# Attention over sorted edges: the first term of a quad's sum goes to PSUM by ScalarE, and VectorE's steps are joined over quads

## What is computed

```python
w_m = (efeat @ W_msg + b_msg).reshape(E, in_f, -1)
w_a = (efeat @ W_attn + b_attn).reshape(E, in_f, -1)
h_src = feat[src][:, :, None]
e1 = w_m * h_src
e2 = w_a * h_src
seg_max = jax.ops.segment_max(e2, dst, num_segments=N)
ex = jnp.exp(e2 - seg_max[dst])
denom = jax.ops.segment_sum(ex, dst, num_segments=N)
attn = ex / denom[dst]
ft = jax.ops.segment_sum(e1 * attn, dst, num_segments=N)
```

## Time and profile before

| | us |
|---|---|
| median of 3 runs (lowest to highest) | 8912.76 (8904.54 to 8920.91) |
| the profiled execution, its own time | 8910.58 |
| its span in the profile | 8908.9 |
| attention blocks (tops copied, first to last start) | 5804.2 to 8779.9 |

### The profile page before, as it was taken

The page is one execution under the profiler, slowest core; times in us unless marked ns, Lnnn a source line. Parts: engine busy times, 40 slices in busy tenths (PEclk is TensorE's granted clock), DMA queues, the critical chain, the costliest instruction groups (busy, mean ns, idle before and its releaser), DMA issues. The chain is left out here.

```text
span 8908.9 us, 135582 instructions
## 1 busy us (share of the span) xinstructions
PE 7159.9 (80%) x35152; PEld 4074.4 (46%) x35152; DVE 7506.5 (84%) x11807; ACT 4804.9 (54%) x7730; POOL 6381.3 (72%) x6335
## 2 busy tenths in 40 slices
PE   3888857888887088888888889488888888888884
PEld 3776744565565055555555555233333333333331
DVE  7999956788888388888888888499999999999997
ACT  5999956666775065665666556233333333333333
POOL 6777767777776677777777777377777777777774
PEclk9989967888888589999999999699999999999997
DMA  4222211111111111111111111122222222222223
GB/s 155 64 62 63 62 42 45 45 46 46 48 46 43 15 29 31 28 33 28 33 28 28 33 28 18 20 72 76 76 76 80 78 76 76 76 76 78 81 76 100
DMA packets 499695, 493.19 MB, mean 55 GB/s; under 512 B 181075, under 2 KB 396906, under 8 KB 498731
## 3 DMA queue, kind: packets, MB, share of 16 engines
q1 hardware_dynamic: 299595, 371.60, 12.4%
q0 software_dynamic: 199904, 119.78, 8.1%
HBM read 240.96 MB, written 249.95 MB: 55 GB/s over the span
## 5 line engine op out<-in xcount | busy, mean ns | idle before, releaser
L2524 POOL DMA_INDIRECT attn_got<-tab,attn_line x1760 | 1912.2, 1086 | 791.6 <-issue 503.5
L1982 POOL DMA_INDIRECT sheaf_got<-tab,sheaf_idx x1612 | 1702.7, 1056 | 488.5 <-issue 470.2
L2577 PE MATMUL attn_q<-attn_X,ident 128*128 128x512 f32 x3520 | 1718.0, 627 | 101.5 <-ACT attn_S L2657 92.5
L2071 PE MATMUL sheaf_acc<-sheaf_hot_hi,sheaf_wide 128*128 128x392 bf16 x6696 | 1355.1, 345 | 283.3 <-DVE sheaf_hot_hi L2274 281.5
L1508 POOL DMA_INDIRECT nnconv_got<-tab,nnconv_idx x1116 | 1081.4, 969 | 381.9 <-issue 321.6
L2577 PEld LDWEIGHTS attn_q<-attn_X,ident 128*128 128x128 f32 x3520 | 652.1, 198 | 1193.5 <-issue 1193.5
L2714 DVE TENSOR_TENSOR attn_T<-attn_w,attn_got 128x1024 f32<-128x1024 f32 x880 | 1052.8, 1217 | 152.0 <-PE attn_w L2568 116.7
L2657 ACT COPY attn_S<-attn_q 128x512 f32<-128x512 f32 x440 | 255.9, 582 | 1531.2 <-PE attn_q L2584 1531.2
L1173 POOL DMA_INDIRECT gcn_got<-tab,gcn_idx x868 | 827.6, 953 | 304.0 <-issue 277.1
L2071 PEld LDWEIGHTS sheaf_acc<-sheaf_hot_hi,sheaf_wide 128*128 128x128 bf16 x6696 | 655.8, 106 | 819.7 <-issue 491.1
L1267 PE MATMUL gcn_acc<-gcn_hot,pieces 128*128 128x512 f32 x2604 | 740.6, 442 | 196.7 <-ACT gcn_hot L1321 134.1
(11 more groups left out here) (508 smaller groups left out, 13676.9 us busy)
## 6 DMA issues: line engine op xcount, KB each, us to landing
sums<-attn_S SPq DMA_DIRECT2D x110, 1024.0 KB, 5.1
tops<-attn_S SPq DMA_DIRECT2D x110, 512.0 KB, 2.9
attn_got<-tab,attn_line POOLq DMA_INDIRECT x1760
sheaf_got<-tab,sheaf_idx POOLq DMA_INDIRECT x1612
gcn_key<-src_key SPq DMA_DIRECT2D x62, 384.0 KB
gcn_blk<-src_blk SPq DMA_DIRECT2D x62, 384.0 KB
nnconv_got<-tab,nnconv_idx POOLq DMA_INDIRECT x1116
nnconv_key<-src_key SPq DMA_DIRECT2D x62, 256.0 KB
```

The lines of the kernel that those rows point to most:

```text
L1982: e.indirect_dma_start(out=got[at.b][:, j, D:D + T2], out_offset=None, in_=tab[2], in_offset=indices(idx[at.b], j)).then_inc(s_got[half][a ...
L2071: mm = e.matmul(pacc[k][:, 0:HH], wide[at.b][half][:, part, col, :], hot[:, k * HH:(k + 1) * HH], start=False, stop=False, skip_group_chec ...
L2524: e.indirect_dma_start(out=got[at.b][:, 4 * q + n, :], out_offset=None, in_=tab[3], in_offset=indices(ids[:, q, n, :], D + 2)).then_inc(s_ ...
L2577: e.matmul(to, ident[:, :], X[:, q, :, n, :], start=n == 0, stop=False)
```

## The change

ScalarE gets a new step, `begin_sum(at, q)`: it copies slot 0 of a quad's weights and weighted products from `X` straight into the bank `pq`. PE then adds only the slots 1 to 3 and the pass on top, with products that never begin a group (start=False); one opening product ahead of the stage starts the bank once. `s_open` and `s_begun` are the semaphores for it. DVE's `larger` over slots is one instruction for four quads where it was two; `below` and `product` are two instructions of two quads each where they were four of one, `below` as a TENSOR_TENSOR subtraction in place of a SCALAR_TENSOR_TENSOR; and their order around `back` changes.

```diff
             def quad_sum(at, q, between=None):
                 to = pq.rearrange("p (t c) -> p t c", t=2)
-                turn_wait(e, s_prod, at.of(QB, q + 1))
-                turn_wait(e, s_state, at.of(QB, q + 2))
-                for n in range(4):
-                    e.matmul(to, ident[:, :], X[:, q, :, n, :], start=n == 0, stop=False)
+                turn_wait(e, s_begun, at.of(QB, q + 1))
+                for n in range(1, 4):
+                    e.matmul(to, ident[:, :], X[:, q, :, n, :], start=False, stop=False, skip_group_check=True)
                     if between and n == 2:
                         between()
...
+            def begin_sum(at, q):
+                e.wait_ge(s_prod, at.of(2, q // 2 + 1))
+                if q > 0 or at.k > 0:
+                    e.wait_ge(s_state, at.of(QB, q + 2))
+                e.copy(pq.rearrange("p (t c) -> p t c", t=2), X[:, q, :, 0, :]).then_inc(s_begun, 1)
...
                 if at.k > 0:
                     put_state(prev, 1)
+                    begin_sum(prev, 2)
                     put_state(prev, 2)
+                    begin_sum(prev, 3)
...
                 tops_out(at)
                 if at.k < NBQ - 1:
                     passing(at.plus(1))
+                begin_sum(at, 0)
                 put_state(at, 0)
+                begin_sum(at, 1)
...
-            def below(q):
-                e.scalar_tensor_tensor(
-                    out=Tb[:, q, 0, :, :], in0=Tb[:, q, 0, :, :], scalar=1.0,
-                    in1=ptop[:, q, None, :].to_broadcast([P, 4, CH]), op0=ALU.mult, op1=ALU.subtract).then_inc(s_sub, 1)
+            def below(half):
+                q = slice(half * QB // 2, (half + 1) * QB // 2)
+                e.tensor_tensor(Tb[:, q, 0, :, :], Tb[:, q, 0, :, :],
+                                ptop[:, q, None, :].to_broadcast([P, QB // 2, 4, CH]),
+                                ALU.subtract).then_inc(s_sub, 1)
...
-                for q in range(QB - 2, -1, -1):
-                    n = back(q)
-                    below(q + 1)
-                    ch.wait(n)
+                n = back(2)
+                ch.wait(n)
+                n = back(1)
+                below(1)
+                ch.wait(n)
+                ch.wait(back(0))
...
                 below(0)
                 if more:
                     times(nxt, 2)
-                product(0)
                 e.wait_ge(s_scale, at.of(1, 1))
...
-                product(1)
+                product(0)
                 if more:
                     times(nxt, 3)
-                product(2)
-                product(3)
+                product(1)
```

More of the change, by code:

```diff
@@ L2457, in gnn_kernel @@
             s_carried, s_pass, s_at, s_mk, s_ids = seml("carried", "pass", "line_at", "mk", "ids")
+            s_begun, s_open = seml("begun", "open")
             s_copied, = seml("copied")
@@ L2549, in _ @@
                     e.wait_ge(s_w, 16 * 5 * (P // RW))
+                    e.matmul(pq[:, :], ident[:, :], Wc[:, :], start=True, stop=True).then_inc(s_open, 1)
                     def turned(at):
@@ L2583, in quad_sum @@
                         before = carried[:, :] if q == 0 else S[at.b][:, q - 1, CH:]
-                        e.matmul(pq[:, :], passes[at.b][:, q, :], before, start=False, stop=True).then_inc(s_quad, 1)
+                        e.matmul(pq[:, :], passes[at.b][:, q, :], before, start=False, stop=False,
+                                 skip_group_check=True).then_inc(s_quad, 1)
                     def step(at):
@@ L2609, in _ @@
                     e.sem_inc(s_state, 2)
+                    e.wait_ge(s_open, 1)
                     def line_index(at):
@@ L2633, in weights @@
                     def weights(at, q):
-                        e.wait_ge(s_sub, at.of(QB, QB))
+                        e.wait_ge(s_sub, at.of(2, 2))
                         if at.k > 0:
@@ L2692, in _ @@
                         put_state(At(NBQ - 1), q)
+                        if q < QB - 1:
+                            begin_sum(At(NBQ - 1), q + 1)
                 @block.vector
@@ L2707, in times @@
                         if q == 0 and at.k >= 2 and 0 in halves:
-                            e.wait_ge(s_prod, at.of(QB, -QB))
+                            e.wait_ge(s_prod, at.of(2, -2))
                         if q % 2 == 0 and 0 in halves:
@@ L2744, in back, with product @@
                                 in1=Sb[:, q, 0:CH], op0=ALU.add, op1=ALU.max))
-                        def below(q):
-                            e.scalar_tensor_tensor(
-                                out=Tb[:, q, 0, :, :], in0=Tb[:, q, 0, :, :], scalar=1.0,
-                                in1=ptop[:, q, None, :].to_broadcast([P, 4, CH]), op0=ALU.mult, op1=ALU.subtract).then_inc(s_sub, 1)
-                        def product(q):
-                            e.wait_ge(s_x, at.of(QB, q + 1))
+                        def below(half):
[3 more added lines that the diff above has]
+                                            ALU.subtract).then_inc(s_sub, 1)
+                        def product(half):
+                            q = slice(half * QB // 2, (half + 1) * QB // 2)
+                            e.wait_ge(s_x, at.of(QB, (half + 1) * QB // 2))
                             e.scalar_tensor_tensor(out=X[:, q, 1, :, :], in0=Tb[:, q, 1, :, :], scalar=1.0,
@@ L2759, in a_block @@
                         e.wait_ge(s_t, at.of(2 * QB, 2 * QB + 2))
-                        for q in range(0, QB, 2):
-                            n = ch.do(larger(two[:, q:q + 2, :, :].rearrange("p q n c -> p q (n c)"),
-                                             Tb[:, q:q + 2, 0, 0:2, :].rearrange("p q n c -> p q (n c)"),
-                                             Tb[:, q:q + 2, 0, 2:4, :].rearrange("p q n c -> p q (n c)")))
+                        n = ch.do(larger(two[:, :, :, :].rearrange("p q n c -> p q (n c)"),
+                                         Tb[:, :, 0, 0:2, :].rearrange("p q n c -> p q (n c)"),
+                                         Tb[:, :, 0, 2:4, :].rearrange("p q n c -> p q (n c)")))
                         if more:
@@ L2811, in _ @@
                         times(At(0), q)
-                    walk(e, NBQ, a_block, ch, 3 + QB + QB - 1, head=4)
+                    walk(e, NBQ, a_block, ch, 2 + QB + QB - 1, head=4)
                     e.wait_ge(s_state, NBQ * QB + 2)
```

## The result

| | median us | runs | profiled span us | mean granted clock | us per attention block |
|---|---|---|---|---|---|
| before | 8916.42 | 8904.54 to 8920.91 | 8908.9 | 0.897 | 27.30 |
| after | 9303.58 | 9298.46 to 9309.89 | 9296.7 | 0.854 | 30.69 |

The change makes the kernel slower, by a ratio of 1.0438 (95% interval 1.0425 to 1.045). The median of before is now over four runs. 9304 lies in the range of 9010 to 9320, 84 us above the 9220 that was forecast.

A forecast was written before the change was run, and what follows sets the result against it. The prediction took a loop of PE's stretch A and VectorE's stretch B as the bound. A 16.01, clock 1.75 and B 12.34 made 30.10 us a block against 27.30, +308 us: 9220, range 9010 to 9320 (0.80).

The forecast's parts named there:

- What bounds the kernel: Attention loop: A from t0 (end of `times(nxt, 2)`) to `times(.., 1)`, 14.84 us; B from there to next t0, 12.20.
- The first copy stands late: ScalarE's quad 0 copy (0.59 us) queues behind the pass matrices; PE starts at t0 + 4.94 instead of t0 + 1.56.
- The second copy: ScalarE's quad 1 copy, 0.59 us behind `put_state`; PE's shortened sum starts at t0 + 11.16, making A 16.01 us.
- The clock: PE's longer pauses leave its clock low in every block for 3.5 us of work, adding 1.75 us to A.
- VectorE in B: The new order of `back` and joined `below` lengthens VectorE's stretch B by 0.14 us, to 12.34.
- The sum: Attention block: 16.01 + 1.75 + 12.34 = 30.10 us against 27.30, +308 us over 110 blocks, 9220 in all.
- The three joins in A save 0.18 us of VectorE's readiness and no time: Joined `larger` and two joined `product` steps in A: VectorE ready 0.18 us earlier, no gain as PE is late.
- the third rival: ScalarE's first copy starts as its data come, at t0 + 2.85; block 27.24 us, 8904 in all; chance 0.05.
- That the clock stays high: PE's clock in attention stays high or as often high as before; block 28.35 us, 9026 in all; chance 0.18.
- That it stays low 5 us or more beyond PE's return, through quad 1's sum: PE's clock costs another 1.75 us a block; 9412 in all, 9316 if one block in two; chance 0.06.
- VectorE as the bound: VectorE bounds attention and PE follows, so joins and removed products gain 1.43 us a block; 8753 in all; chance 0.09.
- GpSimd was written off: GpSimd's gathers in the attention stage were taken as idle in part of each block, with no cost added.

The follow-up runs named there:

- the kernel without joined products: VectorE's joined maxima and `below` on the kernel before, with its four single-quad products kept and no ScalarE copies into the bank: 8910 us.
- joins only: VectorE's joined maxima, `below` and products and their new order on the kernel before, without ScalarE's copies; PE adds all four slots: 9279 us.
- The early copy: The changed kernel with `begin_sum(at, 0)` moved ahead of `tops_out` and `passing`: 9173 us.
- the two fastest kernels: Kernel before with `matrices(at.plus(2), 0)` behind the fourth product and two spare products in PE's pause, without and with ScalarE's copy for quad 1: 8806 and 8795 us.
- joins only with spare products: VectorE's joins without ScalarE's copies, on the kernel before, plus two spare identity products in each of PE's two pauses: 9095 us.
- the last kernel: The changed kernel with its first copy ahead of `tops_out` and `passing`, plus three and two spare products in PE's pauses: 9067 us.
- the moved matrices: Kernel before with `matrices(at.plus(2), 0)` behind the fourth identity product of quad 0 instead of the third: 8913 us; with two spare products, 8806 us.

## Why the prediction came out as it did

- *What bounds the kernel.* Right: a loop of PE's stretch A and VectorE's stretch B. Spare products on the kernel before gave 27.05, its block at full clock. That a shorter A gains down to VectorE's own time was confirmed only once the clock was held (26.26); without it the clock takes such gains back.
- *The first copy stands late.* Right in place and size: t0 + 4.85 for t0 + 4.94, 0.587 us for 0.59. Moving it gave 131 us.
- *The second copy.* Right: from the pass's end (7025.84) to `matrices` (7030.89) 5.05 us, forecast 4.95.
- *The clock.* Right in kind, too small in size: the term was 1.75 us a block and measured 2.29 in A (7.13 less 4.84). It was taken as "as long as it stayed low after it came back", 3.5 us. PE came back at 7014.01 and the clock rose at 7023.25, 9.2 us later: the products of `matrices(nxt, 3)` between two pauses did not raise it. Counted from that return, 3.5 us would have been over before quad 0's start at t0 + 4.94, and A would have lost nothing; the term fits only if the 3.5 us begin with quad 0. From there the clock stayed low for 4.5 us, and half of that is the 2.3 us lost. So the way in which the term was worked out does not hold, and that it came within 0.54 us is partly luck.
- *VectorE in B.* The term was +0.14. A second block of after, DVE's `times`:

```profile
7103.65 2.35 DVE L2730 TENSOR_TENSOR attn_T<-attn_w,attn_got 128x1024 f32<-128x1024 f32 x2
...
7124.38 1.23 DVE L2730 TENSOR_TENSOR attn_T<-attn_w,attn_got 128x1024 f32<-128x1024 f32 x1 [1.79 <-PE attn_w L2570]
...
7134.40 2.35 DVE L2730 TENSOR_TENSOR attn_T<-attn_w,attn_got 128x1024 f32<-128x1024 f32 x2
```

  t0 = 7106.00, A = 7124.38 - 7106.00 = 18.38, and B = 7134.40 + 2.35 - 7124.38 = 12.37, against 12.34 forecast (means 18.34 and 12.38). Right. In the kernel without joined products the block does not show it: A was shorter by as much there, with a clock that was low less often.
- *The sum.* 30.10 forecast, 30.69 measured: +0.54 a block from the clock, +0.10 behind the pass, +0.03 in B, less 0.09 at PE's start. Times 110 that is the miss of 65 us, and the 14 us ahead of the blocks are most of the rest.
- *A step that was incomplete.* "The three joins in A save 0.18 us of VectorE's readiness and no time". True in the changed kernel, where the copy is later still: quad 0 starts at t0 + 4.85, and t0 + 3.18 in joins only. But by this text the joins look harmless, and alone they cost 363 us. The joined product's end at t0 + 2.85 was worked out only for the third rival, and its clock was left at 0.26 us there: the third rival, and the expectation for joins only, failed by the same omission. The early copy shows it: 29.53 measured, where that rival had 27.24.
- *The rivals.* That the clock stays high: no. That it stays low 5 us or more beyond PE's return, through quad 1's sum: it stayed low 9.2 us beyond the return, but only up to `matrices(.., 0)` at 7022.39 and not through quad 1, so that rival's condition came true in part and its price of 9412 did not. VectorE as the bound: no; it becomes true in the two fastest kernels. GpSimd was written off ("idle in part of each block"); that holds for the changed kernel, but GpSimd is the bound in joins only with spare products, and in part of the blocks of the last kernel.

Open: how the clock comes to settle blocks so closely, 27.29 to 27.31 in four kernels with different work in A and B and 30.67 to 30.69 in three. That it is the low clock is shown for before and for the moved matrices, which differ by 0.79 us a block once it is held, and fits the counts of low blocks; why it settles on these two values no run here shows.

## What to carry to other kernels

Where an engine is relieved of work that others wait for, ask what its first instruction now waits for: here a product removed from PE put a copy in front of all of them, behind 6 us of ScalarE's queue, and a joined instruction delivered the first quad only with the second. Two edits can each cost the whole of a loss; take them apart before blaming one. And when an edit that should shorten a loop measures as nothing, look at the granted clock of PE's pauses before concluding that the loop is bound elsewhere: fill the pause with spare products and measure again.

## What the runs showed of the hardware

- PE's clock can hide a gain: the kernel before and one with a shorter PE stretch both came out at 27.3 us, with the clock low in 58 and in 77 of 88 blocks, and with two useless products (1.75 us) in each block they took 27.05 and 26.26. More work made the kernel before 0.3% faster, and the changed one 2.6% faster.
- Low clock does not end with PE's return: in the changed kernel 2.1 us of products between pauses of 3.5 and 2.6 us left it at 0.50, and it was low for 10.2 us in every block.
- An indirect gather on GpSimd takes 0.94 us, and 2.9 when it starts just inside a VectorE instruction of 2.28 us with both operands in SBUF; inside one of the same length with an operand in PSUM it takes 0.94. The mean gather was 1089 ns in the kernel before and as much as 1361 with joined instructions.
- ScalarE writes 512 f32 a partition into PSUM from SBUF in 0.587 us, the same as it reads them back (0.581), and the changed kernel adds its products without a start flag to what ScalarE wrote, in all 110 blocks, after one opening product of the bank.
